# Reordering the second routing front of a hybrid block: row numbers, slots' experts, shared expert and clock fillers

## The chip, the core and the metric

The kernel runs on one core of a Trainium2 chip. The metric is device time in microseconds; the time before is the median of three runs. The core has a matrix engine (TensorE, "PE" in the profile), VectorE ("DVE"), ScalarE ("ACT"), GpSimd ("POOL") and SyncE ("SP"), which issues most DMAs. Each runs its own list of instructions in order, and they wait for one another by semaphores.

## The reference

A batch of 2 sequences of 1024 tokens with 128 channels passes through four residual steps. What is computed, cut to its core:

```python
x = x + attn_a(layernorm(x))   # RWKV-like linear attention
x = x + ffn(layernorm(x))      # first expert layer
x = x + attn_b(layernorm(x))   # hierarchical attention, 16 heads of 64
x = x + ffn(layernorm(x))      # second expert layer, the same weights

def ffn(x):
    shared_out = (silu(x @ shared_gate_w) * (x @ shared_up_w)) @ shared_down_w
    logits = x @ gate_w                      # 32 experts
    topk_ids = argmax(logits)
    xs = x * sigmoid(max(logits))
    sorted_x = xs[argsort(topk_ids)]         # tokens grouped by expert
    d = (silu(sorted_x @ gate_e) * (sorted_x @ up_e)) @ down_e
    return shared_out + d[inverse order]
```

## The kernel before, in words

Tokens lie in four chunks of 512 (c = 0 to 3), each of four tiles of 128. The kernel runs four stages in a row on every engine: `a_*`, the first expert layer `f_*` with k = 0, `b_*`, and the second expert layer `f_*` with k = 1. Each stage is a hand-written list per engine, so the order of the work is the order of the calls in the code.

Stage b takes 16 units (`UNITS`; a unit is a pair of heads of one sequence; `LAST` is 15). Per unit TensorE computes scores in two parts (fine and coarse, `scores`, L1755), VectorE subtracts maxima and transposes (`soften`, L2021), ScalarE takes exponents (L1935, L1939), TensorE forms the weighted sums (`weighted`, L1804) and their weights' sums (L1785 in the last unit), VectorE takes reciprocals (`divide`, L2038 to L2045), ScalarE copies the numerators (`copy_y`, L1954), GpSimd multiplies the two (L2204, two halves of 512 columns), TensorE projects (`project_out`, L1825), and VectorE adds the projection to the tokens (`gather_out`, L2054). The last two units are added in one gather per half.

The second expert layer has a front that overlaps the end of stage b. Chunks 0 and 1 are ready early and are routed during stage b. Chunks 2 and 3 come with the last unit. Per chunk: statistics on VectorE (`front_statistics`, L967 to L974), a power on GpSimd (L178), normalised rows (chunk 2 on ScalarE, L987; chunk 3 on VectorE, L1365), turns on TensorE (`front_turn`, L997), copies on ScalarE (L1002), logits (`front_logits`, L1007) and the choice of the expert on VectorE (`route`, L1026 to L1033), which writes a one-hot table. TensorE counts tokens from that table (`count_tokens`, L1090 and L1091).

Rows of tokens are then scattered into `sorted_x` in DRAM, grouped in slots of 32 rows per expert. The row numbers come in two halves of eight tiles, both on VectorE. For chunks 0 and 1 these are `first_slots` (L1109 to L1113) and `first_rows` (L1117, L1118, then L1099 to L1101). For chunks 2 and 3 it is `second_places` (L1125 to L1135, again L1099 to L1101). Its end (L1137 to L1143) finds the expert of each slot. GpSimd issues 16 indirect DMAs (`scatter`, L1469): eight wait for the first half's numbers, eight for the second's. When all 16 have landed, SyncE reads slots back (L1525). TensorE turns the rows (`turn_in`, L1197) and starts the loop over 24 steps of four slots (`gate_up`, L1251, and on).

Among all this lies the shared expert: `shared_half` (L1156, two matmuls of 512 columns on TensorE), `gate_shared` (L1172, ScalarE), `product_shared` (L1178, VectorE), `shared_out` (L1165, 16 matmuls) and `add_shared` (L1183, VectorE), for each chunk. The loop's first turn stands behind the last of it in TensorE's list. `keep_clock` (L1193) issues matmuls whose results nobody reads.

The order on VectorE in front of the loop is: `divide`, `first_slots`, gather, statistics, gather, statistics, `row_ids` (L1073), `first_rows`, chunk 3's rows, two products of chunk 0, `route` of chunks 2 and 3 in one call, `add_shared` of chunk 0, `second_places` with the slots' experts, two products of chunk 1, slot numbers. On TensorE it is: last projection, two shared halves of chunk 0, turns of chunks 2 and 3, logits of both, `shared_out` of chunk 0, `count_tokens`, two shared halves of chunk 1, `keep_clock(2)`, a shared half of chunk 2, the slots' row (L1218), and the rest of the shared expert.

Of the kernel before, what the change touches and what calls it, by code (L numbers as in the profile page):

```python
# [51 lines left out]
SLOT_BOUND = "second_places keeps the expert of a slot between 0 and EXPERTS - 1"  # L52
# [38 lines left out]
def hybrid_block(nc, w, out):  # L91
    with ExitStack() as ctx:
# [1028 lines left out]
        def second_places(dve, chain, k):  # L1121
# [14 lines left out]
            row_numbers(dve, chain, a, 1)  # L1136
            chain(dve.tensor_scalar(before.cmp[:, 0:EXPERTS], before.taken, place_col[:, 1:2], None, ALU.is_le))  # L1137
# [47 lines left out]
        def f_pe(pe, k):  # L1185
# [20 lines left out]
            else:  # L1206
                front_turn(pe, k, 2)
                front_turn(pe, k, 3)
                front_logits(pe, k, 2)
                front_logits(pe, k, 3)  # L1210
                shared_out(pe, k, 0)
            count_tokens(pe, k, 1)
            shared_half(pe, k, 1, 0, 1)
            shared_half(pe, k, 1, 1, 2)
            keep_clock(2)
# [70 lines left out]
        def f_act(act, k):  # L1286
# [5 lines left out]
            if k == 0:  # L1292
                front_copy(act, k, 3)
            else:
                gate_shared(act, k, 0, 0)
                front_norm(act, k, 2)
                gate_shared(act, k, 0, 1)
                front_copy(act, k, 2)
                front_copy(act, k, 3)
# [50 lines left out]
        def f_dve(dve, chain, k):  # L1350
# [8 lines left out]
            else:  # L1359
                row_ids(dve, k)  # L1360
                first_rows(dve, chain, k)
# [6 lines left out]
            if k == 1:  # L1368
                for n in range(2):
                    product_shared(dve, k, 0, n)  # L1370
                route(dve, chain, k, 2, 2)
# [5 lines left out]
            add_shared(dve, k, 0)  # L1377
            second_places(dve, chain, k)
            for n in range(2):
                product_shared(dve, k, 1, n)  # L1380
# [206 lines left out]
        for b in range(BATCH):  # L1587
# [8 lines left out]
            "acc logits_in").split()}  # L1596
# [95 lines left out]
        def b_pe(pe):  # L1692
# [8 lines left out]
            def keep_busy(times):  # L1701
                for _ in range(times):
                    pe.matmul(Y[0], ident, const[:, 0:CHUNK], start=True, stop=True)

# [113 lines left out]
            def project_out(n):  # L1818
                pe.wait_ge(wo_in[n % 2], 16 * (n // 2) + 16)
                for i in range(SEQ // P):  # L1820
                    if i % 4 == 0:
                        pe.wait_ge(h["normed"], 2 * n + i // 4 + 1)
# [22 lines left out]
            for n in range(UNITS + 1):  # L1845
# [7 lines left out]
                if new:  # L1853
# [3 lines left out]
                    project(n + 1, 1, 1)  # L1857
                if now:
                    scores(n, ROUGH)
                if new:  # L1860
# [26 lines left out]
                else:  # L1887
                    project_out(n - 1)
                    pe.wait_ge(h["y_out"], UNITS)
                    for half in range(2):  # L1890
                        shared_half(pe, 1, 0, half)
# [107 lines left out]
        def b_dve(dve, chain):  # L1999
# [48 lines left out]

            def gather_out(n, j):
# [39 lines left out]
            for n in range(0, UNITS + 1):  # L2089
# [14 lines left out]
                if n == UNITS:  # L2104
                    first_slots(dve, chain, 1)
# [278 lines left out]
```

## Time and profile before

| | us |
|---|---|
| median of three runs | 557.3 (556.14 to 558.34) |
| profiled execution, its own time | 555.4 |
| span of that execution in the trace | 553.5 |

All moments below are microseconds from the span's start. In a timeline the first two numbers are the start and the length of an instruction (or of a group of neighbours, with their count behind x); in brackets stand the idle time of the engine before it and what ended it. In the chain of waits each piece follows from the one above it.

### The profile page before, as it was taken

What the parts mean: (1) busy time and instruction counts of PE and PEld (TensorE: products, weight loads), DVE (VectorE), ACT (ScalarE), POOL (GpSimd) and SP (SyncE); (2) the same over time, 40 slices, a digit from 0 to 9 for tenths busy, and PEclk for the clock granted to TensorE, in tenths of its full rate; (3) what the DMA queues carried; (4) which work ended last, traced back from release to release, by engine and by line L of the source; (5) the groups of instructions that cost most, each with busy time, mean ns of one, the idle gap of its engine ahead of it and who ended that gap; (6) DMA issues with size and microseconds to landing.
All of it is one profiled execution on the core that took longest, in us unless ns stands there. A gap on an engine that the chain in (4) does not pass through costs nothing.

```text
span 553.5 us, 16703 instructions
## 1 busy us (share of the span) xinstructions
PE 497.8 (90%) x6472; PEld 306.0 (55%) x6472; DVE 422.3 (76%) x979; ACT 290.9 (53%) x624; POOL 250.7 (45%) x294
## 2 busy tenths in 40 slices
PE   6989888887989988999999999999999868989991
PEld 3323232355445544777767777777767656544540
DVE  3386968987757776878898888899878987747762
ACT  3544344254358864656545555546644433448870
POOL 3556777555614454253344443333233434534442
PEclk9999999999999998999999999999999987899997
DMA  6799820000269962100000000000000000169964
GB/s 183 313 426 285 95 26 0 2 0 20 81 195 271 279 203 68 31 3 21 21 21 22 23 21 22 22 21 21 22 21 8 7 2 16 37 191 275 277 215 139
DMA packets 45326, 54.11 MB, mean 98 GB/s; under 512 B 10880, under 2 KB 36416, under 8 KB 44224
## 3 DMA queue, kind: packets, MB, share of 16 engines
q1 hardware_dynamic: 42688, 47.78, 29.7%
q0 software_dynamic: 2560, 5.26, 2.7%
q8 instruction: 52, 0.85, 0.6%
q14 instruction: 26, 0.21, 0.2%
HBM read 43.55 MB, written 9.48 MB: 96 GB/s over the span
## 4 chain that ended last, share of the span: by engine, by line
PE 61%; DVE 23%; issue 6%; DMA 3%; POOL 3%; ACT 3%; SPq 0%; DVEq 0%; POOLq 0%; ACTq 0%
PE psum L1251 9%; PE psum L1732 7%; PE psum L1750 7%; PE psum L1825 5%; PE psum L1804 4%; PE psum L1270 4%; PE psum L1258 3%; DVE arena L761 3%; POOL sorted_x L1469 2%; PE psum L1773 2%; DVE arena L755 2%; PE psum L277 2%; PE psum L278 2%; DVE arena L2034 2%; DVE arena L2029 2%
## 5 line engine op out<-in xcount | busy, mean ns | idle before, releaser
L2204 POOL TENSOR_TENSOR arena<-arena 128x512 f32<-128x512 f32 x32 | 40.9, 1301 | 108.7 <-issue 102.1
L1497 POOL DMA_INDIRECT y_tok<-arena,to x48 | 46.4, 967 | 64.0 <-ACT arena L1320 62.8
L1920 ACT ACTIVATE arena<-psum 128x512 f32<-128x512 f32 x64 | 37.9, 597 | 45.2 <-PE psum L1732 42.0
L1732 PE MATMUL psum<-arena 128*128 128x512 f32 x128 | 59.2, 605 | 0.8 <-ACT arena L1903 0.7
L1251 PE MATMUL psum<-experts,arena 128*32 x96 | 50.2, 605 | 1.0 <-ACT arena L1310 1.0
L1251 PE MATMUL psum<-arena 128*32 128x512 f32 x288 | 50.9, 605 | 0.0
L661 POOL TENSOR_TENSOR arena<-arena 128x512 f32<-128x512 f32 x32 | 37.2, 1179 | 26.2 <-DVE arena L761 17.5
L1750 PE MATMUL psum<-arena 128*128 128x128 f32 x384 | 47.5, 279 | 1.5 <-ACT arena L1925 1.5
L1750 PEld LDWEIGHTS psum<-arena 128*128 128x128 f32 x384 | 45.2, 192 | 2.5 <-ACT arena L1925 2.5
L2141 POOL TENSOR_TENSOR arena<-arena 128x256 f32<-128x256 f32 (+4 forms) x75 | 33.8, 451 | 24.6 <-ACT arena L1939 17.9
L1732 PEld LDWEIGHTS psum<-arena 128*128 128x128 f32 x128 | 23.0, 190 | 35.5 <-issue 34.0
L1334 ACT ACTIVATE arena<-experts 128x768 f32 x48 | 40.1, 839 | 2.0 <-issue 1.8
L1393 DVE COPY arena<-psum 128x256 f32<-128x256 f32 x48 | 20.4, 425 | 25.4 <-PE psum L1258 25.0
L1469 POOL DMA_INDIRECT sorted_x<-arena,row x32 | 31.1, 970 | 19.3 <-DVE row L1101 10.7
L761 DVE TENSOR_TENSOR_SCAN arena<-psum,arena 128x512 f32<-128x512 f32 x32 | 39.1, 1269 | 0.0
L1804 PE MATMUL psum<-arena 64*64 64x64 f32 (+2 forms) x1728 | 37.1, 225 | 2.2 <-ACT arena L1935 1.5
L1928 ACT ACTIVATE arena<-psum 128x512 f32<-128x512 f32 x48 | 28.7, 598 | 16.4 <-PE psum L1750 16.4
L1270 PEld LDWEIGHTS psum<-experts,arena 128*32 128x32 f32 x192 | 20.6, 110 | 30.1 <-issue 29.8
L1804 PEld LDWEIGHTS psum<-arena 64*64 64x64 f32 x1728 | 33.2, 138 | 6.3 <-ACT arena L1935 1.6
L1825 PE MATMUL psum<-arena 128*128 128x128 f32 x256 | 34.4, 288 | 2.3 <-POOL arena L2204 2.3
L2054 DVE TENSOR_TENSOR x_tok<-x_tok,psum 128x512 f32<-128x512 f32 x30 | 20.6, 687 | 20.4 <-PE psum L1825 20.2
L755 DVE TENSOR_TENSOR arena<-arena,psum 128x512 f32<-128x512 f32 x32 | 19.9, 685 | 19.2 <-PE psum L293 19.1
(240 smaller groups left out, 1204.7 us busy)
## 6 DMA issues: line engine op xcount, KB each, us to landing
arena<-in_experts SPq DMA_DIRECT2D x48, 384.0 KB, 4.2
experts<-in_experts SPq DMA_DIRECT2D x8, 1536.0 KB, 17.3
arena<-sorted_x SPq DMA_DIRECT2D x48, 64.5 KB, 3.6
sorted_x<-zeros SPq DMA_DIRECT2D x2, 1536.0 KB, 13.7
arena<-in_w_qkv SPq DMA_DIRECT2D x16, 192.0 KB, 3.2
arena<-y_tok SPq DMA_DIRECT2D x8, 256.0 KB, 3.1
x_tok<-in_x SPq DMA_DIRECT2D x4, 256.0 KB, 4.5
arena<-in_w_out SPq DMA_DIRECT2D x16, 64.0 KB, 1.9
```

Source lines behind the costliest of these rows:

```text
L761: dve.tensor_tensor_scan(a_state[:, m, 1:CHUNK + 1], DECAYS[:, :], a_kv[m % HALF], a_state[:, m, 0:1], ALU.mult, ALU.add).then_inc(s["stat ...
L1251: mm = pe.matmul(bank[2 + s % 2][rows, :], f_gxt[s % 2][:, rows], weights, start=True, stop=True)
L1270: mm = pe.matmul(bank[6 + s % 2][SLOT_ROWS * j:SLOT_ROWS * j + SLOT_ROWS, 0:C], f_sht[s % 2][:, rows], weights, start=(half == 0), stop=(h ...
L1334: act.activation(f_w_act[s % 5], experts[:, bass.ds(expert_at[s], WROW)], ACT.Copy).then_inc(t["w_act"], 1)
L1469: pool.indirect_dma_start(out=sorted_x[k], out_offset=bass.IndirectOffsetOnAxis(ap=f_row[:, i:i + 1], axis=0), in_=row_of(k, i), in_offset ...
L1497: pool.indirect_dma_start(out=y_tok, out_offset=bass.IndirectOffsetOnAxis(ap=f_to[:, s:s + 1], axis=0), in_=f_gy[(s + 4) % 8], in_offset=N ...
L1732: pe.matmul(ring("in", n, j)[:, :], b_w[n % 2][:, which * P:which * P + P], x, start=True, stop=True)\
L1750: mm = pe.matmul(ring("in", n, 5 + i // 4)[:, i % 4 * P:i % 4 * P + P], x, b_w[n % 2][:, 2 * P:3 * P], start=True, stop=True)
L1804: mm = pe.matmul(place(Y[r][out]), b_v[n % 2][rows, i, out], e[rows, head, i - part.start, cols], start=(i == 0), stop=last_place(r, i, cols))
L1825: mm = pe.matmul(ring("out", n, i // 4)[:, i % 4 * C:i % 4 * C + C], b_yn[:, i * P:i * P + P], b_wo[n % 2], start=(n < LAST - 1 or n < LAS ...
L1920: act.activation((b_q, b_k)[which][:, part * CHUNK:part * CHUNK + CHUNK], src, ACT.Copy, scale=(D_B ** -0.5, 1.0)[which]).then_inc(h["drai ...
L2204: pool.tensor_tensor(b_yn[:, part], b_y[:, part], b_rec[:, part], ALU.mult).then_inc(h["normed"], 1)
```

## The change

Only the second front (k = 1) and the last unit of stage b change their order. For k = 0 the calls stay as they were.

- TensorE: fillers (matmuls whose results nobody reads) ahead of and behind the last unit's coarse scores. The last projection stands between the two shared halves of chunk 0, with three fillers behind. Turn and logits come chunk by chunk. A shared half of chunk 1 stands ahead of the counting, `shared_out` of chunk 0 behind it. `keep_clock` goes.
- VectorE: it normalises the second half of the last unit in place of GpSimd (`normalise_late`), and takes a product of chunk 0 there. `first_slots` moves behind the statistics, `first_rows` behind chunk 3's rows. After the routing come one product, `second_places`, `slot_experts` (cut out of `second_places`), and only then the add of chunk 0 and the products of chunk 1.
- ScalarE: the second gate of chunk 0 ahead of chunk 2's rows.
- GpSimd: one multiply less in the last unit.

The diff, without two lines that only rename and some context:

```diff
@@ second_places
             row_numbers(dve, chain, a, 1)
+
+        def slot_experts(dve, chain, k):
+            before, a = half_of(k, 0), half_of(k, 1)
             chain(dve.tensor_scalar(before.cmp[:, 0:EXPERTS], before.taken, place_col[:, 1:2], None, ALU.is_le))
...
@@ f_pe
             else:
                 front_turn(pe, k, 2)
+                front_logits(pe, k, 2)
                 front_turn(pe, k, 3)
-                front_logits(pe, k, 2)
                 front_logits(pe, k, 3)
+                shared_half(pe, k, 1, 0, 1)
+            count_tokens(pe, k, 1)
+            if k == 0:
+                shared_half(pe, k, 1, 0, 1)
+            else:
                 shared_out(pe, k, 0)
-            count_tokens(pe, k, 1)
-            shared_half(pe, k, 1, 0, 1)
             shared_half(pe, k, 1, 1, 2)
-            keep_clock(2)
+            if k == 0:
+                keep_clock(2)
             shared_half(pe, k, 2, 0)
             done(pe, "slot_col", 1)
@@ f_act
                 gate_shared(act, k, 0, 0)
+                gate_shared(act, k, 0, 1)
                 front_norm(act, k, 2)
-                gate_shared(act, k, 0, 1)
                 front_copy(act, k, 2)
@@ f_dve
                 row_ids(dve, k)
-                first_rows(dve, chain, k)
...
             ins.then_inc(t["xn_last"], 1)
             if k == 1:
+                first_rows(dve, chain, k)
+                route(dve, chain, k, 2, 2)
+                product_shared(dve, k, 0, 1)
+                second_places(dve, chain, k)
+                slot_experts(dve, chain, k)
+                add_shared(dve, k, 0)
                 for n in range(2):
-                    product_shared(dve, k, 0, n)
-                route(dve, chain, k, 2, 2)
+                    product_shared(dve, k, 1, n)
             else:
                 route(dve, chain, k, 2, 1)
                 for n in range(2):
                     product_shared(dve, k, 0, n)
                 route(dve, chain, k, 3, 1)
-            add_shared(dve, k, 0)
-            second_places(dve, chain, k)
-            for n in range(2):
-                product_shared(dve, k, 1, n)
+                add_shared(dve, k, 0)
+                second_places(dve, chain, k)
+                slot_experts(dve, chain, k)
+                for n in range(2):
+                    product_shared(dve, k, 1, n)
@@ b_pe
+            def fill_wait(cols):
+                for at in range(0, cols, CHUNK // 2):
+                    pe.matmul(ring("out", LAST - 1, 0)[:, 0:CHUNK // 2], ident, const[:, 0:CHUNK // 2], start=True, stop=True)
@@ project_out
                     if i % 4 == 0:
-                        pe.wait_ge(h["normed"], 2 * n + i // 4 + 1)
+                        if n == LAST and i:
+                            pe.wait_ge(h["normed_late"], 1)
+                        else:
+                            pe.wait_ge(h["normed"], 2 * n + i // 4 + 1)
@@ b_pe, loop over units
+                if n == LAST:
+                    pe.wait_ge(h["acc"], 2 * (LAST - 1))
+                    fill_wait(CHUNK + CHUNK // 2)
                 if now:
                     scores(n, ROUGH)
+                if n == LAST:
+                    fill_wait(CHUNK)
...
                 else:
+                    pe.wait_ge(h["y_out"], UNITS)
+                    shared_half(pe, 1, 0, 0)
                     project_out(n - 1)
-                    pe.wait_ge(h["y_out"], UNITS)
-                    for half in range(2):
-                        shared_half(pe, 1, 0, half)
+                    shared_half(pe, 1, 0, 1)
+                    pe.wait_ge(h["z_out"], UNITS)
+                    for _ in range(3):
+                        pe.matmul(bank[7], ident, const[:, 0:CHUNK], start=True, stop=True)
@@ b_dve
+            def normalise_late():
+                part = slice(CHUNK, SEQ)
+                dve.wait_ge(h["y_out"], UNITS)
+                dve.wait_ge(h["o"], 2 * LAST)
+                dve.tensor_tensor(b_yn[:, part], b_y[:, part], b_rec[:, part], ALU.mult).then_inc(h["normed_late"], 1)
@@ b_dve, loop over units
                 if n == UNITS:
-                    first_slots(dve, chain, 1)
+                    normalise_late()
+                    product_shared(dve, 1, 0, 0)
...
                     route(dve, chain, 1, n - PAIRS - 4, 1)
+            first_slots(dve, chain, 1)
             dve.wait_ge(h["acc"], 2 * LAST)
@@ b_pool_engine
-                for j in range(2):
+                for j in range(2 if n < LAST else 1):
```

## Rows read from the trace of the kernel before

**Rows 1.** The page, part 4: shares of the chain that ended last, by engine.

```profile
PE 61%; DVE 23%; issue 6%; DMA 3%; POOL 3%; ACT 3%; SPq 0%; DVEq 0%; POOLq 0%; ACTq 0%
```

**Rows 2.** Chain of waits in order of time, 479 to 495: start, length, what.

```profile
479.02 0.18 DVE row L1101
...
488.88 2.68 DMA sorted_x<-arena,row
...
494.25 0.31 PE psum L1197
```

**Rows 3.** Timeline of GpSimd, 454 to 481: start, length, line, operation, [idle before].

```profile
454.48 2.91 POOL L2204 TENSOR_TENSOR arena<-arena 128x512 f32<-128x512 f32 x2 [2.23 <-DVE arena L2045]
...
462.90 1.25 POOL L178 TENSOR_TENSOR arena<-arena,const 128x4 f32<-128x4 f32 x1 [1.18 <-DVE arena L974]
465.91 1.10 POOL L1469 DMA_INDIRECT sorted_x<-arena,row  x1 [1.77 <-DVE row L1101]
...
474.90 0.97 POOL L1469 DMA_INDIRECT sorted_x<-arena,row  x1 [0.30 <-issue]
480.03 0.96 POOL L1469 DMA_INDIRECT sorted_x<-arena,row  x1 [4.16 <-DVE row L1101]
```

**Rows 4.** Timeline of VectorE, 458 to 482.

```profile
458.41 0.69 DVE L2054 TENSOR_TENSOR x_tok<-x_tok,psum 128x512 f32<-128x512 f32 x1
...
462.86 0.42 DVE L1117 TENSOR_TENSOR arena<-arena 128x256 f32<-128x256 f32 x1
...
464.96 1.11 DVE L1365 TENSOR_SCALAR arena<-x_tok,arena 128x128 f32<-128x128 f32 x4
...
469.65 0.42 DVE L1026 TENSOR_REDUCE arena<-psum 128x8 f32<-128x256 f32 x1 [2.40 <-PE psum L1007]
...
473.90 0.19 DVE L1125 TENSOR_TENSOR psum<-psum,arena 128x32 f32<-128x32 f32 x1
...
477.44 0.43 DVE L1135 TENSOR_TENSOR arena<-arena 128x256 f32<-128x256 f32 x1
...
480.36 1.29 DVE L1178 TENSOR_TENSOR arena<-arena,psum 128x512 f32<-128x512 f32 x2
```

**Rows 5.** Lines L1109 and L1094 over the span: min, median, max in ns.

```profile
L1109 DVE TENSOR_TENSOR_SCAN arena<-const,psum x1: 689/689/689, 124.0 to 124.0; 128x256 f32<-128x256 f32 x1
L1109 DVE TENSOR_TENSOR_SCAN arena<-const,arena x1: 1331/1331/1331, 455.0 to 455.0; 128x256 f32<-128x256 f32 x1
...
L1094 DVE TENSOR_SCALAR arena<-arena x4: 189/190/1096, 124.7 to 474.9; 128x32 f32<-128x32 f32 x4
```

**Rows 6.** Timeline of TensorE, 443 to 494 (an fp32 matmul stands as two).

```profile
443.92 0.30 PE L1767 MATMUL psum<-attend_bf 64*64 64x256 bf16 x4 [1.59 <-DVE arena L2029]
...
446.20 3.26 PE L1804 MATMUL psum<-arena 64*64 64x64 f32 x103 [1.51 <-ACT arena L1935]
...
455.90 3.62 PE L1825 MATMUL psum<-arena 128*128 128x128 f32 x16 [2.29 <-POOL arena L2204]
...
464.06 0.66 PE L997 MATMUL psum<-const,arena 128*128 128x128 f32 x4 [0.66 <-ACT arena L987]
...
469.43 3.76 PE L1165 MATMUL psum<-shared_down,arena 128*128 128x128 f32 x16
...
477.11 1.88 PE L1193 MATMUL psum<-shared_up,const 128*128 128x512 f32 x4
...
481.70 2.05 PE L1165 MATMUL psum<-shared_down,arena 128*128 128x128 f32 x16 [0.69 <-DVE arena L1178]
...
493.42 0.31 PE L1197 MATMUL psum<-const,arena 128*128 128x128 f32 x1
```

**Rows 7.** Busy time by stretch: PE, PEld, DVE, ACT, POOL, then granted clock, DMA share, GB/s.

```profile
446.80:450.00 3.20, 3.06 (x107) 2.87 (x105) 3.10 (x6) 0.81 (x3) 0.28 (x1) 0.50 0.02 5
...
467.20:474.00 6.80, 6.80 (x31) 6.42 (x31) 2.88 (x8) 3.38 (x9) 5.16 (x6) 0.50 0.16 55
```

**Rows 8.** Timeline of ScalarE at 452.

```profile
452.35 1.02 ACT L1954 ACTIVATE arena<-psum 128x1024 f32<-128x1024 f32 x1 [4.40 <-POOL arena L2204]
```

More of the change, by code:

```diff
@@ L51 @@
 FOUND = 4
-SLOT_BOUND = "second_places keeps the expert of a slot between 0 and EXPERTS - 1"
+SLOT_BOUND = "slot_experts keeps the expert of a slot between 0 and EXPERTS - 1"
 ROW = C + 1
@@ L1595, in hybrid_block @@
             "shift xn xt x pooled packed packed_odd ready coarse proj drained scored subbed turned expd weighed merged summed y_out z_out divided normed o biased "
-            "acc logits_in").split()}
+            "acc logits_in normed_late").split()}
         w_in, wo_in, bias_in = [sem(f"b_w_in{r}") for r in range(2)], [sem(f"b_wo_in{r}") for r in range(2)], sem("b_bias_in")
```

## Prediction

> **What bounds the kernel now.** I read the page first: TensorE heads the chain that ended last [rows 1], yet the change touches only the stretch between the last attention unit (from about 442 us) and the start of the second expert loop (495 us). The loop behind it runs at one pace per slot, so what counts is when it starts. The profiled execution took 555.4 us for a span of 553.5 us; the median of the runs is 557.3 us, 1.9 above it. Differences are worked out on the span and taken off the median.
>
> Followed backwards, the loop starts when a slot's rows have been read back; that waits for the last of 16 scatters, landed 2.68 us after its issue; and the second eight scatters waited for the second half's row numbers, written at 479.02 [rows 2]. GpSimd stood idle for 4.16 us ahead of them, at 480.03. A scatter takes 1.26 us (eight starts from 465.91 to 474.90, the first 0.15 longer) [rows 3]. TensorE reached the first slot's turn at 493.42, 0.8 us ahead of the turn at 494.25 that waited for the read-back [rows 2, 6]. Two chains of almost equal length end here, **scatters** and **shared expert**: the change pays only if both get shorter.
>
> **Last unit.** TensorE runs at 0.50 of its clock (the 1.2 GHz level) from 446.8 to 450.0, behind a hole in which it waited 1.59 us for VectorE and one of 1.51 us for ScalarE [rows 6, 7]. The added fillers (three of 256 columns ahead of the coarse scores, two behind) sit in these holes. Two of 512 columns took 1.88 us [rows 6], so a 256 one is about 0.47: 1.4 and 0.9 us, less than either hole. They cost nothing while the clock is full; at half clock the first three would take 2.8 us and push the scores back by 1.2. If the clock stays full, 3.2 us of work at half rate could shrink by up to 1.6, and the last divide comes earlier. But ScalarE's copy of the last numerators (452.35, 1.02 us) waits for GpSimd, not for this work [rows 8]: behind it, at 453.4, TensorE now does the first shared half (two 512 matmuls, 1.88 us at most) and starts the last output projection at 455.2 instead of 455.90 [rows 6]. I take **0.7 us** (ends 0 and 0.7; above it the copy binds).
>
> **Gathers.** Today the first half's slot counts lie on VectorE between its divide and the first gather at 458.41, though the projection's first half was there at about 457 [rows 4, 6]. The change puts the late normalise and one shared product there (0.65, half of the two in 1.29 [rows 4]; the normalise has no row: 0.65 as the nearest of its shape on VectorE, 1.45 as one of GpSimd's two in 2.91 [rows 3]; I take 0.65, and with either it is done ahead of the projection's second half at 456.2). Half of 16 matmuls of that shape at 2.05 us [rows 6] puts the first gather at 456.25: **2.16 us earlier** (1.46 if the 0.7 fails). From there to the end of the row ids, with the second gather and the statistics, it is 4.45 us today (458.41 to 462.86) [rows 4].
>
> Behind the projection TensorE does the second shared half (to about 459.1) and three fillers of 512 columns (2.8 us at 0.94 each, to 461.9). Chunk 2's turn, at 464.06 today, waits for ScalarE's rows and comes due 2.16 earlier, at 461.9 [rows 6]: nothing lost at full clock, up to 3 us of lateness for the logits at half clock. ScalarE's second gate moves ahead of those rows; its input is there from 458.2 and the shift it now precedes comes at 460, so it costs nothing.
>
> **Slot counts and first row numbers.** The counts now stand between the statistics and the row ids. In the second front they took 3.44 us beside a GpSimd multiply; the first front shows their scan at 0.69 instead of 1.33 and the first small operation at 0.19 instead of 1.10 [rows 5]. Without the multiply that is 3.44 - 0.64 - 0.91 = 1.9 us; its ends are 1.9 and 3.44, and I take 1.9, as only a short GpSimd power is beside it. So the row ids end at 456.25 + 4.45 + 1.9 = 462.6. Then the last chunk's rows, 1.11 us [rows 4]: 463.7, **2.35 us earlier** than 466.07. Then the first row numbers, 2.10 (462.86 to 464.96): 465.8, **0.85 us later** than today.
>
> What that power (1.25 us from 462.90) does to VectorE the trace shows: the 256-wide add at 462.86 took 0.42 us beside it, and the one at 477.44, with GpSimd idle, 0.43 [rows 3, 4]. I charge nothing. Against this stands a rule: the Trainium skill, GPSIMD Engine Reference, section Specifications, says that GpSimd shares its SBUF interfaces with VectorE, with contention for VectorE instructions in a two-port mode or with two SBUF inputs. By that rule the moved counts could lose some 0.65 us beside the power, an estimate, and the sum would be 0.65 us worse; the rows beside the multiply bear it out, the add beside the power does not.
>
> **Scatters.** GpSimd starts 0.95 us after the row numbers (464.96 to 465.91) [rows 3, 4]: 466.75. Nothing separates the two eights now, if the second row numbers come in time: the last of 16 starts 1.41 + 14 x 1.263 = 19.1 us later, at 485.85, against 488.88 [rows 2, 3]: **3.0 us earlier**. Landing and read-back stay as they are; the weight loads ahead of them move along.
>
> Do the second row numbers come in time? With turns and logits of chunks 2 and 3 one by one, chunk 3's turn starts at about 464.2 behind chunk 2's logits (TensorE's order, where today VectorE's rows set it), and its own logits end at about 466.6; today both sets, partly at half clock, hold VectorE until 469.65 [rows 4, 7]. The two-chunk routing (2.35 us, 469.65 to 472.0) ends at 469.0. Its call still takes both chunks at once: "one by one" holds for turns and logits alone. Counting no longer waits behind the shared output (3.76 us from 469.43 [rows 6]); the second places start at 469.65, behind one shared product, and take 5.2 (473.90 to 479.1) [rows 2, 4]: 474.9, so that GpSimd could issue at 475.8. It is busy with the first eight until 477.0. So **1.2 us of slack**: late next is the queue of GpSimd, not the routing.
>
> **Shared expert.** Slots' experts 1.25, one add 0.69, two products 1.29: the second product ends at 478.1 instead of 481.65 [rows 4], and the second shared output starts then instead of at 481.70, 3.6 earlier. The 11.7 us behind it (to 493.42) keep their order and end at 489.8; the scatters then bind, at 494.25 - 3.0 = 491.25 [rows 2, 6]. The two clock fillers that go (1.88 us, hidden in a wait) leave TensorE with hardly any work from 475.1 to 478.1. A half-clock stretch costs half its length: 3.2 us cost 1.6, 6.8 us (467.2 to 474.0) cost 3.4 [rows 7]. The 1.45 us between the two chains cover the first but for 0.15, not the second. Ends 0 and 3.4; I charge nothing.
>
> **Sum.** 3.0 us off: span 550.5, execution 552.4, median 557.3 - 3.0 = **554.3 us**. A measurement of this kernel tells about 0.5% (2.8 us) from no change, so the forecast lies just beyond that edge. Its own range: 552.8 (landing quicker, as fewer weight loads are in flight) to 555.9 (slot counts at their upper end, 1.55 more).
>
> **Rivals.**
> First, **the front stays slow**: the clock gains nothing (0.7) or the counts stay at 3.44 (1.55), or both. The row numbers come up to 2.25 us later, and all 16 scatters with them: 555.0 to 556.5. For it: the slow rows lie beside GpSimd work, and some is left. Against: the first front's rows. Chance 0.2.
> Second, **the shared chain ends last**, because the clock falls in the 3 us hole that the fillers left: with 3.4 us lost TensorE is at its first turn at 493.2, 0.2 earlier than today, so 557.1; with 1.6 to 2.5 lost 554.5 to 556.2. For it: the stretch from 467.2 to 474.0. Against: the other low stretch lasted 3.2 us. Chance 0.17.
> Third, **slower**: the same fall, but the low clock reaches into the loop, whose matmuls then run another 6.8 us at half rate, 3.4 us lost on top of the second rival's end: 560.5. It decides once the low stretch lasts past the loop's start at 491.9. For it: with 6.8 us behind 478 the clock is back only 7 us ahead of that, and a hole of its own may follow. Against: both of today's low stretches ended under dense work, and the shared expert's from 481.70 on is dense [rows 6, 7]. Chance 0.1.
> Fourth, more than forecast: both chains short and the landing quick: 552.2. Chance 0.08.
>
> **How the numbers follow.** The forecast has 0.45. The range 552.0 to 557.6 leaves out the slower case and some tail below. Faster by over 0.5% (under 554.5): two thirds of the forecast's case, the fourth, and the mild ends of the first two, 0.42; slower by over 0.5%: 0.11, the third and a little of what no case names; within: 0.47.
>
> **What would show it.** Right: the granted clock stays full from 446 to 460; the first gather at about 456.3; slot counts in 1.9 us; the first scatter at about 466.8 and sixteen without a pause, the last at 485.9; TensorE's second turn waiting for the read-back, the loop starting about 492. Wrong: a pause in the scatters (routing late), a first scatter after 468, half clock behind 477, or turns that no longer wait for data. If the loop's own pace changes, the sum is void.

## The result and the profile after

The changed kernel takes 554.49 us (median of 6 runs, 553.68 to 555.91) beside 557.54 us for the kernel before on the same chip: a ratio of 0.9949, 95% interval [0.9928, 0.9971]. The forecast was 554.3 us, so the time is right. The trace shows that part of the way there was another one. One of all the executions below, of the kernel called e12, was slow (639.32 us at a granted clock of 0.748), and its median and ratio leave that one out.

The profiled execution after took 554.11 us for a span of 552.2 us (555.4 and 553.5 before). I measure the **front** from the start of the last unit's coarse scores (443.92 before, 444.07 after) to the loop's first `gate_up` (494.98 before, 493.51 after): 51.06 us became 49.44 us. The stretch behind it is 58.5 us before and 58.7 us after.

Shares of the chain that ended last, as in [rows 1]:

```profile
PE 64%; DVE 21%; issue 7%; ACT 3%; DMA 3%; POOL 2%; DVEq 0%; POOLq 0%; SPq 0%; ACTq 0%
```

The chain of waits of the kernel after, in order of time (start, length, what), to set beside [rows 2]:

```profile
465.79 1.16 PE psum L1007 x8
466.95 3.41 PE psum L1159 x4
470.36 0.11 PE psum L1090
...
475.85 0.17 DVE row L1101
...
477.78 1.29 DVE arena L1181 x2
...
479.11 2.72 PE psum L1168 x16
481.84 4.43 PE psum L1159 x8
486.27 1.78 PE psum L1168 x16
...
492.67 0.11 PE psum L1200
492.78 0.31 PE psum L1200
```

Before, the scatters, their landing and the read-back stood at the end. None of them is in this chain. TensorE's shared expert (L1159, L1168) runs through to the first turns (L1200) with no wait for a DMA. The other chain is still close: SyncE issues the read-back at 490.36, 1.2 us earlier than before, and the first slot's rows land some 1.8 us later, just ahead of the turns at 492.50.

GpSimd after, beside [rows 3]:

```profile
453.75 1.28 POOL L2239 TENSOR_TENSOR arena<-arena 128x512 f32<-128x512 f32 x1 [1.34 <-PE psum L1844]
...
461.05 1.31 POOL L178 TENSOR_TENSOR arena<-arena,const 128x4 f32<-128x4 f32 x1 [1.18 <-DVE arena L974]
466.98 1.08 POOL L1481 DMA_INDIRECT sorted_x<-arena,row  x1 [4.62 <-DVE row L1101]
...
473.43 1.19 POOL L1481 DMA_INDIRECT sorted_x<-arena,row  x1 [0.30 <-issue]
...
477.56 0.96 POOL L1481 DMA_INDIRECT sorted_x<-arena,row  x1 [0.30 <-issue]
...
486.42 0.96 POOL L1481 DMA_INDIRECT sorted_x<-arena,row  x1 [0.30 <-issue]
```

The 4.16 us pause between the two eights is gone: 477.56 is the ninth scatter. The first starts 1.07 us later than before, the last 2.46 us earlier (486.42 against 488.88 in [rows 2]).

VectorE after, beside [rows 4] and [rows 5]:

```profile
454.24 1.34 DVE L2080 TENSOR_TENSOR arena<-arena 128x512 f32<-128x512 f32 x1
455.60 0.69 DVE L1181 TENSOR_TENSOR arena<-arena,psum 128x512 f32<-128x512 f32 x1
456.56 0.69 DVE L2087 TENSOR_TENSOR x_tok<-x_tok,psum 128x512 f32<-128x512 f32 x1 [0.27 <-PE psum L1844]
...
460.88 0.69 DVE L1109 TENSOR_TENSOR_SCAN arena<-const,arena 128x256 f32<-128x256 f32 x1
461.60 0.19 DVE L1094 TENSOR_SCALAR arena<-arena 128x32 f32<-128x32 f32 x1
...
462.76 0.23 DVE L1073 TENSOR_SCALAR arena<-const,place_col 128x8 f32<-128x8 f32 x1
462.90 1.11 DVE L1371 TENSOR_SCALAR arena<-x_tok,arena 128x128 f32<-128x128 f32 x4
...
466.99 0.42 DVE L1026 TENSOR_REDUCE arena<-psum 128x8 f32<-128x256 f32 x1 [0.88 <-PE psum L1007]
...
470.62 0.20 DVE L1125 TENSOR_TENSOR psum<-psum,arena 128x32 f32<-128x32 f32 x1 [0.58 <-PE psum L1091]
```

The gather waits 0.27 us for TensorE's projection, not for VectorE's own work. The counts take 1.88 us (460.88 to 462.76) where they took 3.44. The routing starts at 466.99, not at 469.65.

ScalarE's copy of the last numerators after, beside [rows 8]:

```profile
452.50 1.02 ACT L1981 ACTIVATE arena<-psum 128x1024 f32<-128x1024 f32 x1 [4.40 <-POOL arena L2239]
```

TensorE after, beside [rows 6], and its granted clock, beside [rows 7] (busy time of PE, PEld, DVE, ACT and POOL, then clock, DMA share, GB/s):

```profile
446.35 1.16 PE L1820 MATMUL psum<-arena 64*64 64x64 f32 x64 [0.28 <-ACT arena L1962]
...
455.40 1.95 PE L1844 MATMUL psum<-arena 128*128 128x128 f32 x16
457.18 1.88 PE L1159 MATMUL psum<-arena,shared_up 128*128 128x512 f32 x4
458.90 2.74 PE L1918 MATMUL psum<-const 128*128 128x512 f32 x6
...
466.76 3.60 PE L1159 MATMUL psum<-arena,shared_up 128*128 128x512 f32 x4
...
479.11 2.72 PE L1168 MATMUL psum<-shared_down,arena 128*128 128x128 f32 x16 [1.41 <-DVE arena L1181]
481.63 4.64 PE L1159 MATMUL psum<-arena,shared_up 128*128 128x512 f32 x8
```

```profile
446.00:450.00 4.00, 3.08 (x180) 2.87 (x183) 3.86 (x7) 1.11 (x4) 0.12 (x1) 1.00 0.01 4
450.00:466.00 16.00, 13.62 (x116) 9.03 (x107) 14.35 (x45) 6.59 (x11) 6.02 (x5) 1.00 0.00 1
...
467.00:470.00 3.00, 3.00 (x4) 1.07 (x5) 2.76 (x6) 0.60 (x4) 2.39 (x3) 0.50 0.11 39
...
480.30:481.00 0.70, 0.70 (x6) 0.70 (x6) 0.00 (x0) 0.00 (x0) 0.70 (x1) 0.50 0.29 94
...
483.00:483.70 0.70, 0.70 (x2) 0.34 (x1) 0.00 (x0) 0.12 (x1) 0.58 (x1) 0.50 1.02 315
```

The fillers sit in what were holes, and the clock is full from 446 to 466. It is at 0.50 (the 1.2 GHz level) from about 467 to 470, and once more from 480.3 to 483.7. The second stretch follows the place where `keep_clock` stood until the change: TensorE waits 1.52 us ahead of the slots' row (477.32) and 1.41 us ahead of the second `shared_out` (479.11), and the clock falls 1.2 us into that.

### The profile page after: what moved, and what is told of

Same layout as the page of the kernel before. It is cut to its first block, busy times and chain, and to the rows that moved or that the text cites. A ratio compares the mean times of both kernels' runs of the same rounds, so it can differ in the third digit from the quotient of the medians.

```text
span 552.2 us, 16726 instructions
## 1 busy us (share of the span) xinstructions
PE 496.9 (90%) x6484; PEld 303.2 (55%) x6484; DVE 422.4 (76%) x980; ACT 291.0 (53%) x624; POOL 249.2 (45%) x293
## 4 chain that ended last, share of the span: by engine, by line
PE 64%; DVE 21%; issue 7%; ACT 3%; DMA 3%; POOL 2%; DVEq 0%; POOLq 0%; SPq 0%; ACTq 0%
PE psum L1258 9%; PE psum L1766 7%; PE psum L1748 7%; PE psum L1844 5%; PE psum L1820 4%; PE psum L1277 4%; PE psum L1265 3%; DVE arena L761 3%; PE psum L1789 3%; DVE arena L755 2%; PE psum L277 2%; PE psum L1159 2%; PE psum L278 2%; PE psum L1168 2%; DVE arena L2105 2%
## 5 line engine op out<-in xcount | busy, mean ns | idle before, releaser
L2239 POOL TENSOR_TENSOR arena<-arena 128x512 f32<-128x512 f32 x31 | 39.2, 1285 | 108.0 <-issue 102.4
L661 POOL TENSOR_TENSOR arena<-arena 128x512 f32<-128x512 f32 x32 | 37.2, 1181 | 26.2 <-DVE arena L761 17.5
L1766 PE MATMUL psum<-arena 128*128 128x128 f32 x384 | 47.5, 278 | 1.5 <-ACT arena L1952 1.5
L1820 PE MATMUL psum<-arena 64*64 64x64 f32 (+2 forms) x1728 | 35.9, 221 | 1.5 <-ACT arena L1966 1.2
L1844 PE MATMUL psum<-arena 128*128 128x128 f32 x256 | 33.0, 281 | 0.4 <-issue 0.4
```

The lines of the kernel that those rows point to most:

```text
L661: pool.tensor_tensor(a_g[m % HALF], a_r[c % 2], a_state[:, m, 0:CHUNK], ALU.mult).then_inc(s["g"], 1)
L1766: mm = pe.matmul(ring("in", n, 5 + i // 4)[:, i % 4 * P:i % 4 * P + P], x, b_w[n % 2][:, 2 * P:3 * P], start=True, stop=True)
L1820: mm = pe.matmul(place(Y[r][out]), b_v[n % 2][rows, i, out], e[rows, head, i - part.start, cols], start=(i == 0), stop=last_place(r, i, cols))
L1844: mm = pe.matmul(ring("out", n, i // 4)[:, i % 4 * C:i % 4 * C + C], b_yn[:, i * P:i * P + P], b_wo[n % 2], start=(n < LAST - 1 or n < LAS ...
L2239: pool.tensor_tensor(b_yn[:, part], b_y[:, part], b_rec[:, part], ALU.mult).then_inc(h["normed"], 1)
```

## Experiments

For each kernel the table gives moments of one profiled execution, in us from the start of the last unit's coarse scores ("front" is the loop's start), and the time of the runs with its ratio to the kernel before on the same chip. The rows were timed on several chips, where the medians of the kernel before lay between 556.92 and 557.54 us. So a cost between two rows is taken from their ratios below; as each ratio has an interval of about 0.2% to either side, such a cost is uncertain by some 1.5 us.

| kernel | first scatter | second row numbers end | last scatter starts | read-back issued | shared expert ends | front | median, ratio [interval] |
|---|---|---|---|---|---|---|---|
| before | 21.99 | 35.27 | 44.96 | 47.66 | 49.66 | 51.06 | |
| e1 before | 22.08 | 35.21 | 44.90 | 47.51 | 49.60 | 50.92 | |
| e11 before | 22.08 | 35.20 | 44.89 | 47.71 | 49.59 | 50.90 | |
| after | 22.91 | 31.95 | 42.35 | 46.29 | 48.59 | 49.44 | 554.49, 0.9949 [0.9928, 0.9971] |
| e2 after | 22.91 | 32.10 | 42.47 | 45.71 | 48.72 | 49.28 | |
| e5 first rows back | 21.89 | 34.74 | 44.42 | 49.28 | 51.39 | 52.40 | 556.89, 1.0 [0.9988, 1.0012] |
| e6 no unit fillers | 23.71 | 32.75 | 43.13 | 45.96 | 49.39 | 50.11 | 555.74, 0.9992 [0.9973, 1.0011] |
| e10 no wide fillers | 22.92 | 34.49 | 44.18 | 47.65 | 49.46 | 50.80 | 556.27, 0.999 [0.9971, 1.0009] |
| e3 `keep_clock` back | 22.94 | 31.71 | 42.10 | 45.76 | 46.68 | 48.86 | 553.53, 0.9944 [0.9926, 0.9962] |
| e4 a weight load later | 22.90 | 31.94 | 42.33 | 45.12 | 48.57 | 49.13 | 554.39, 0.995 [0.9933, 0.9967] |
| e7 both of these | 22.92 | 31.95 | 42.34 | 44.62 | 46.92 | 47.89 | 553.66, 0.9942 [0.9924, 0.996] |
| e8 GpSimd normalises | 22.92 | 31.13 | 42.01 | 44.72 | 46.10 | 47.92 | 553.31, 0.9934 [0.9914, 0.9955] |
| e12 the same again | 22.91 | 33.21 | 42.90 | 47.41 | 48.18 | 50.69 | 554.23, 0.995 [0.993, 0.9971] |
| e9 three edits | 22.91 | 31.13 | 41.99 | 45.17 | 47.09 | 48.35 | 554.28, 0.9951 [0.9932, 0.997] |

**Both kernels once more (e1, e2, e11).** The times fell by 3.05 us, the front of the profiles by 1.6. Does the front vary, or does something ahead of it?

> The kernel of before, unchanged, profiled a second time. Its first profile (555.4 us) lies below all its timed runs (556.1 to 558.8), while that of the changed kernel (554.1) lies among its own (553.7 to 555.9). If the trace of before that the prediction used was simply a lucky one, this profile comes out at 556 to 558 us, with more low-clock time than 0.974 allowed, most of it between 442 and 495 us (theory A: the change removes clock losses that vary from run to run). If before's runs differ elsewhere (theory B: another stage, or the time around the span), the stretch 442 to 495 is the same within 0.5 us and the difference lies outside it.

> The changed kernel a second time. Theory A: the stretch from 442 us to the loop's start repeats within 1 us, as its clock is held by fillers up to 466. Low-clock stretches behind 466 and behind 479 should be there again, perhaps shifted. Time 553.7 to 555.9 us.

> The kernel before once more, for a third profile. The front between the last unit's coarse scores and the loop took 51.06 and 50.92 us in two profiles of it, and 49.44 and 49.28 in two of the kernel after, 1.6 us apart, while the timed medians lie 2.5 to 3 apart. If the rest is the spread of what lies ahead of the front, the front repeats within 0.2 us and the coarse scores start somewhere between 443.9 and 445.8; if the front itself varies, it shows 52 or more.

Measured: the front of the kernel before repeats within 0.16 us in three executions, that of the kernel after within 0.16 us in two. The coarse scores start at 443.92, 445.30 and 445.77 in the kernel before, at 444.07 and 444.52 in the kernel after, and up to 446.03 in the others, whose code ahead of them is the same. So what lies ahead moves by some 2 us from execution to execution, and the front's own 1.6 us is clear of the spread of these five profiles. (The pair e8 and e12 below shows a larger spread.)

**The first row numbers back to their place (e5).**

```diff
                 row_ids(dve, k)
+                first_rows(dve, chain, k)
...
             if k == 1:
-                first_rows(dve, chain, k)
                 route(dve, chain, k, 2, 2)
```

> The changed kernel with the first half's row numbers back ahead of chunk 3's rows on VectorE. Working from the changed kernel's rows: the row numbers move 1.0 us earlier (to about 465.1 us), chunk 3's rows 2.1 us later, the routing and the second row numbers 1.5 to 2.1 later (478.0). If the forecast's account is right (16 scatters in a row, 1 to 1.5 us of slack for the routing), the first scatter starts 1.0 earlier, a pause of 1.5 to 2.0 us comes between the eights, and the last scatter starts within 0.7 us of the changed kernel's, later rather than earlier. The shared expert's chain moves 1.5 to 2.0 later and ends last: time 1 to 2 us above the changed kernel's. Rival: if the early start of the first eight is what counts, the last scatter starts 1 us earlier and the time falls by up to 1 us.

Measured: 556.89 us at a ratio of 1.0, the whole gain gone. The two rows of TensorE for chunk 3's turn and logits in e5, and GpSimd's scatters:

```profile
466.12 1.12 PE L997 MATMUL psum<-const,arena 128*128 128x128 f32 x4 [1.54 <-DVE arena L1372]
467.92 1.91 PE L1007 MATMUL psum<-gate_w,arena 128*128 128x32 f32 x8 [0.69 <-ACT arena L1002]
```

```profile
474.90 0.95 POOL L1481 DMA_INDIRECT sorted_x<-arena,row  x1 [0.30 <-issue]
479.61 0.95 POOL L1481 DMA_INDIRECT sorted_x<-arena,row  x1 [3.76 <-DVE row L1101]
```

The first scatter is 1.0 us earlier and the ninth 2.1 us later. Chunk 3's rows come behind the numbers, TensorE waits 1.54 us for them, and behind that wait the clock is at 0.51 (466 to 470), so that turn and logits take nearly twice as long. I had expected the last scatter to lose at most 0.7 us, and it lost 2.1; the clock was left out of that. Against the coarse scores chunk 3's turn starts 1.7 us later than in the kernel after and its logits end 2.9 us later: 1.7 are the order, the other 1.2 the clock, and the run does not part the two in the time. In this profile the read-back is issued 4.86 us after the last scatter (3.94 after), so its front of 52.40 is not the order's alone either. Still, this is the part on which the change rests: a later first eight for an earlier second eight.

**Without the fillers of the last unit (e6).**

```diff
-                if n == LAST:
-                    pe.wait_ge(h["acc"], 2 * (LAST - 1))
-                    fill_wait(CHUNK + CHUNK // 2)
                 if now:
                     scores(n, ROUGH)
-                if n == LAST:
-                    fill_wait(CHUNK)
```

> The changed kernel without the fillers around the last unit's coarse scores. The forecast gave them 0.7 us (0 to 0.7). If right: half clock from about 447 to 450 again, the last sum 0.8 us later, the last projection's start 0 to 0.7 us later (the copy of the numerators binds otherwise), and the first scatter as much later. Rival: nothing moves behind the projection, as the copy and the first shared half set it in either case; then the fillers are worth nothing here: no change in the scatters' start beyond 0.1 us.

TensorE in e6:

```profile
447.27 1.55 PE L1820 MATMUL psum<-arena 64*64 64x64 f32 x64 [1.51 <-ACT arena L1957]
...
457.04 2.02 PE L1844 MATMUL psum<-arena 128*128 128x128 f32 x16 [0.54 <-POOL arena L2234]
```

The 1.51 us hole is back, the clock averages 0.62 from 446.9 to 450.9 (as far behind the coarse scores as 446 to 450 in the kernel after, where it is 1.00), and the projection starts 12.05 behind the coarse scores instead of 11.33. These 0.72 us go on to the loop (50.11 against 49.36, the mean of the two profiles after). By the ratios (0.9992 for 0.9949) the runs lose 2.4 us, more than this front shows, though not beyond the uncertainty.

**Without the three wide fillers (e10).**

```diff
                     shared_half(pe, 1, 0, 1)
-                    pe.wait_ge(h["z_out"], UNITS)
-                    for _ in range(3):
-                        pe.matmul(bank[7], ident, const[:, 0:CHUNK], start=True, stop=True)
```

> The kernel after without the three 512-column fillers behind the last projection and the second shared half. Theory that they hold the clock: the granted clock falls between 461 and 467, turns and logits come later (second choice of the expert by 0.5 to 2 us), the first scatter stays at 22.9 behind the coarse scores, the shared expert ends later or at the same time; time 0 to 1 us above the kernel after. Theory that they only cost TensorE's time: turn 2 and the logits keep their starts, since ScalarE's rows set them, the clock is full there anyway, and the time stays within 0.5.

TensorE's timeline and its stretches in e10:

```profile
464.17 0.66 PE L997 MATMUL psum<-const,arena 128*128 128x128 f32 x4 [3.14 <-ACT arena L987]
465.51 1.91 PE L1007 MATMUL psum<-gate_w,arena 128*128 128x32 f32 x8 [0.69 <-ACT arena L1002]
...
470.74 3.76 PE L1159 MATMUL psum<-arena,shared_up 128*128 128x512 f32 x4
```

```profile
460.00:464.00 4.00, 1.02 (x3) 0.19 (x1) 3.73 (x21) 2.13 (x5) 2.02 (x2) 1.00 0.00 0
464.00:468.00 4.00, 3.15 (x16) 2.84 (x16) 3.76 (x13) 0.71 (x2) 0.31 (x1) 0.59 0.00 0
468.00:472.00 4.00, 3.31 (x12) 2.47 (x11) 1.05 (x4) 1.88 (x2) 2.44 (x3) 0.50 0.09 31
```

Behind the 3.14 us wait the clock falls for the whole routing: both sets of logits take 1.91 us instead of 1.08 and 1.16, and the second row numbers come 2.5 us later than in the kernel after. The first scatter stays (22.92), a 2.2 us pause between the eights is back, and the runs are at 0.999 of before, by the ratios 2.3 us above the kernel after where 0 to 1 was expected. That is not one profile's chance: the mean granted clock of each of its ten executions is 0.968 to 0.980, of the six of the kernel after 0.981 to 0.984. The theory that these fillers hold the clock stands; that they only take TensorE's time falls.

**The clock fillers back, a weight load later, and both (e3, e4, e7).**

```diff
-            if k == 0:
-                keep_clock(2)
+            keep_clock(2)
```

```diff
-            for s in range(4):
+            for s in range(4 - k):
...
                 fetch(s)
+                if k == 1 and s == 3:
+                    weights(3)
```

> The changed kernel with the two clock fillers of the second front put back (between chunk 1's second shared half and chunk 2's first). Theory S (the shared expert ends last, because TensorE's clock falls in the hole from 475 to 479 us): full clock behind 479, the first slot's turn 1.0 to 1.7 us earlier, and the time 0.3 to 1.2 us less than the changed kernel's, as the read-back follows closely. Theory R (the scatters and the read-back end last): the first turn comes earlier too, but the loop does not start earlier by more than 0.3 us, as the second turn then waits for data; no change in time.

> The changed kernel with the fourth of the four weight loads that SyncE issues ahead of the scatters' wait moved behind the first four read-backs, in the second front alone. The last scatter landed 3.9 us after its issue in the changed kernel and 2.7 in the one before. If the weight loads in flight cause that, three quarters of their bytes should let the last scatter land 0.8 to 1.3 us earlier. Theory S: the loop's start does not move by more than 0.3 us, since the shared expert ends last. Theory R: it starts 0.5 to 1.2 us earlier, and so does the end.

> The changed kernel with both edits of the last two experiments: the two clock fillers back and the fourth weight load behind four read-backs. The fillers alone let the shared expert end 1.1 us ahead of the data; the later load alone let the last scatter land 0.8 us earlier but the shared expert ended last. If the two chains bind in turn, together they give what neither gave alone: first turn about 0.8 us earlier than with the fillers alone, loop start 1.2 to 1.5 us ahead of the changed kernel's, time 0.5 to 0.9 us below that with the fillers alone. If something else binds (the slots' weights, say), no less than with the fillers alone.

TensorE in e3, from the second `shared_out` on:

```profile
479.07 2.05 PE L1168 MATMUL psum<-shared_down,arena 128*128 128x128 f32 x16 [1.02 <-DVE arena L1181]
480.96 3.60 PE L1159 MATMUL psum<-arena,shared_up 128*128 128x512 f32 x8
...
491.93 0.78 PE L1200 MATMUL psum<-const,arena 128*128 128x128 f32 x2 [0.98 <-DMA arena<-sorted_x]
```

2.05 and 3.60 us instead of 2.72 and 4.64: the clock is full there, the shared expert ends 1.9 us earlier than after, and the turn waits for the read-back again. So in the kernel after, with `keep_clock` gone and the clock low, the shared expert ended last. But the front gains only 0.5 us of it, because the read-back is next. One pair of profiles doesn't settle that the removal brings the fall: without `keep_clock` the clock fell there in five profiles (after, e2, e4, e5, e6) and stayed at 1.00 in three (e8, e10, e12), behind waits of 1.0 to 1.6 and 1.41 us in all of them; with it, it stayed in all three (e3, e7, e9). In e4 the read-back was issued 0.6 to 1.2 us sooner and the loop's start hardly moved (49.13): shared expert again. That sooner read-back is what the theory of the weight loads asked for (2.79 us after the last scatter, and 2.28 in e7, against 3.94, 3.24 and 3.66 in after, e2 and e3). But e6 and e8, with all four loads ahead, have 2.83 and 2.71, so it isn't shown that the load did it. With both edits the front is 47.89, 1.5 us shorter than after. One step of the loop then took 2.58 us where 1.92 is usual, so that from the coarse scores to the end 1.0 us is left (107.2 for 108.1); the span shows none of it (552.6 for 552.2), as what lies ahead took 1.4 us longer in that execution. Of the three, no time can be told from that of the kernel after.

**GpSimd normalises the second half again (e8, e12).**

```diff
-                        if n == LAST and i:
-                            pe.wait_ge(h["normed_late"], 1)
-                        else:
-                            pe.wait_ge(h["normed"], 2 * n + i // 4 + 1)
+                        pe.wait_ge(h["normed"], 2 * n + i // 4 + 1)
...
-                    normalise_late()
...
-                for j in range(2 if n < LAST else 1):
+                for j in range(2):
```

> The changed kernel with the last unit's second half normalised by GpSimd again, as in the kernel before; all else stays. The late normalise took VectorE 1.34 us beside GpSimd's multiply (twice the 0.65 that the forecast took), and VectorE then still waited 0.27 us for the projection. If VectorE's list is what sets the first gather, the gather comes 0.2 us earlier or so at most; GpSimd's second half ends at about 456.3, when TensorE has just done the projection's first half, so the second gather is not later either: no change (within 0.3 us) in the first scatter's start. Rival: GpSimd's second half comes late by its usual 1.3 to 1.45 us, the projection waits, and the second gather and all behind it come up to 0.7 us later.

> Once more the kernel after with GpSimd normalising the last unit's second half. In six kernels with that multiply on VectorE TensorE waits 0.57 us ahead of chunk 2's turn and the granted clock falls behind chunk 3's logits; in the two with it on GpSimd the wait is 0.40 to 0.43 and the clock stays full up to the loop. Theory that the multiply's place decides this: the clock is 1.00 from 466 to 484 again, the second row numbers come 31.1 behind the coarse scores (31.95 in the kernel after), the loop starts 47.7 to 48.4 behind them, and the time is 553 to 553.8. Theory that the two were chance: the clock falls between 466 and 470, row numbers at 31.7 or later, loop 49 or later, time 554 to 555.

The first scatter stands at 22.92 and 22.91, as after: the multiply's move to VectorE is worth nothing to it. In e8 the clock stayed full from 466 to 484, and I took that for the edit's doing. The second execution says otherwise. Chunk 3's logits and the last landing in e8:

```profile
467.42 1.08 PE L1007 MATMUL psum<-gate_w,arena 128*128 128x32 f32 x8 [0.69 <-ACT arena L1002]
```

```profile
487.72 2.69 DMA sorted_x<-arena,row
```

and in e12, the same code:

```profile
466.17 1.92 PE L1007 MATMUL psum<-gate_w,arena 128*128 128x32 f32 x8 [0.69 <-ACT arena L1002]
```

```profile
487.36 4.49 DMA sorted_x<-arena,row
```

The stretch from 466 to 472, first e8, then e12 (the clock is the third figure from the end):

```profile
466.00:472.00 6.00, 4.37 (x24) 2.54 (x24) 4.82 (x12) 2.89 (x6) 2.75 (x3) 1.00 0.07 23
466.00:472.00 6.00, 5.83 (x15) 3.52 (x16) 3.31 (x8) 2.79 (x8) 3.71 (x4) 0.50 0.11 34
```

The same instructions in the same order gave fronts of 47.92 and 50.69. The difference is a clock of 0.50 from 466 to 472 and a landing that took 1.8 us longer. So the multiply's place alone doesn't decide it. What does stays open: the profiled execution of e12 was the slowest of its eleven (557.03 us, median 554.23), but the mean granted clock is 0.984 to 0.986 in all four executions of e8 and 0.978 to 0.984 in the eleven of e12, on another chip. In the twelve executions of e9, on one chip, it is 0.978 to 0.987, so that executions of one program on one chip differ as much; whether the chip adds to that is not shown.

**Three edits together (e9).** GpSimd normalises, `keep_clock` is back, and the slot numbers stand ahead of chunk 1's products:

```diff
                 add_shared(dve, k, 0)
+                slot_numbers()
                 for n in range(2):
```

> The kernel after with three edits: GpSimd normalises the second half again, the two clock fillers behind the counting are back, and the slot numbers stand ahead of chunk 1's two products on VectorE, so that SyncE's weight loads start about 1.2 us earlier. Theory S (behind the change the shared expert's chain ended last, and with the fillers back the read-back does): the scatters stay as they are, the last 42.2 to 42.4 us behind the last unit's coarse scores; the weight loads are done before the last scatter lands, which then takes 2.8 us or less; the loop starts 47.5 to 47.9 behind those scores (49.44 in the kernel after) and the time is 552.5 to 553.3. If the loop's tail pays back what the front gains (as one look had it, 0.66 us), 553.3 to 554. Theory that the landing is set by the scatters themselves and not by the weight loads beside them: landing stays above 3 us, the loop starts at 48.3 or later.

Measured: 554.28 us and a front of 48.35, where 47.5 to 47.9 was expected; by its ratio this version can't be told from the kernel after. The weight loads were issued 1.28 us earlier against the coarse scores (34.86 for 36.14) and the landing still took 3.16 us. The theory that the loads beside it set the landing has no support in this run.

## Why the prediction was right, and where it was not

**The last unit, 0.7 us: right.** The projection starts at 455.40 (455.2 forecast), 0.65 us earlier against the coarse scores than before; without the fillers 0.72 us are lost. ScalarE's copy stands at 452.50, 8.43 us behind the coarse scores as in the kernel before [rows 8]: it is what caps this gain, as the text said.

**The gather at 456.25: 456.56.** The normalise was taken as 0.65 and took 1.34 us, beside GpSimd's multiply (453.75 to 455.03). That is the direction of the rule weighed in the prediction (the Trainium skill, GPSIMD Engine Reference, Specifications). The longer normalise cost nothing: the gather waited for the projection, as the text said for either value, and starts at the same distance in e8.

**The counts, 3.44 to 1.9 us: 1.88, right.** Here that rule does not show: the scan takes 0.69 us and the small operation 0.19 with GpSimd's power beside them (461.05, 1.31 us). The scan began 0.17 us ahead of that power, the small operation within it. The first numbers and the first scatter (466.98 for 466.75) carry on only the gather's 0.3 us.

**Sixteen scatters without a pause: right,** though the last starts at 486.42, not at 485.85: 0.23 us from the start, the rest mostly from two issues of 1.19 and 1.08 us. The slack of the second places was 0.6 us rather than 1.2, since their end came at 476.02, not 474.9. The low clock from 467 to 470 had eaten into it through `count_tokens`, which stands behind a shared half of 3.60 us (466.76) where e8 shows 1.97.

**The three wide fillers, "nothing lost": half right.** They cost nothing, but the step put their worth at nothing too. The forecast's logits at 466.6 hang on them: without them the runs lose some 2.3 us.

**The clock behind the removed `keep_clock`, charged at nothing (ends 0 and 3.4): wrong.** This term failed, and it is rival 2's mechanism. Two of the text's own signs of being wrong came with it: half clock behind 477, and turns that no longer wait for data. The second `shared_out` was to start at 478.1 and started at 479.11, as the second places came late. From there the low stretch added 0.67 us (2.72 for 2.05) and 1.04 us (4.64 for 3.60). The first turn, forecast at 489.8, came at 492.50: 2.7 us late, more than the 1.45 us between the chains. (Rival 2's upper price is too high: with 3.4 us lost the first turn at 493.2 is 1.95 us behind the forecast's 491.25, so about 556.3 by the sum's own measure and not 557.1, and the third rival's 560.5 falls by as much.)

**Landing unchanged at 2.68 us: wrong in the profiled execution.** From the last issue to the read-back it is 3.94 us, and 3.24 in e2. Over all kernels it is 2.28 to 4.86 us, and 2.71 and 4.51 in one and the same kernel (e8, e12). What sets it stays open.

**The other rivals.** The front did not stay slow (clock full from 446 to 466, counts 1.88), so the first falls. The third's low clock in the loop's beginning is not there: the clock is 1.00 from 493.51 to 497.5, and the stretch behind the front kept its length within 0.2 us. It can come: in e12 the clock is 0.54 from 496 to 498 and 0.61 from 498 to 500, inside the loop, and that stretch takes 60.0 us. The fourth's quick landing did not come.

**The sum.** With both, the front gained 1.6 us where 3.0 were summed. The median fell by 3.05 us, 2.5 against the median of 557.03 us over 19 other runs of the kernel before. So the forecast time was hit in part by luck: two terms of the sum failed, and about 1 us of the timed gain is in no profile. It is no more than what a profiled execution differs from the next in this family (2.8 us between e8 and e12), and 1.6 us lies inside the ratio's interval at its end of 0.9971. Settling it would take many profiles of both kernels; it stays open.

The parts don't add up: taken away singly, first rows, wide fillers and unit fillers cost 2.8, 2.3 and 2.4 us by the ratios, 7.5 together, against a gain of 2.8 by the same measure. Each opens a wait or a low clock on the same chain; that this hides what the others save is likely but not shown, as no run takes away two at once.

## What to carry to other kernels

Order two batches of numbers by what the second one waits for: the queue that consumes the first batch gives the second time, and a later start of the first costs less than a pause between them. When a filler on TensorE is removed or added, price the clock of the work behind it and not the filler's own time; here that was some 2.3 us for fillers that seemed free. And take a second profile of a kernel before explaining a front by one: two executions of the same code lay 2.8 us apart.

## What was unexpected in the hardware

- The granted clock is not fixed by the instructions' order. In e8 and e12 TensorE waited 0.40 and 0.41 us ahead of chunk 2's turn and 0.69 us ahead of either set of logits; then the clock stayed at 1.00 in the one and was 0.50 from 466 to 472 in the other. The two executions were on different chips.
- A VectorE multiply of 128x512 out of two SBUF tiles took 1.34 us beside a GpSimd multiply of that size; the product that follows it, with GpSimd idle and one operand in PSUM, took 0.69. The slow one ended 0.55 us behind the GpSimd multiply (455.58 for 455.03). Beside a GpSimd power of 128x4 a VectorE scan, begun just ahead of it, and four small operations begun within it lost nothing (0.69, and 0.18 to 0.22 us; the last three took the same in the kernel before with GpSimd idle).
- The last of 16 indirect scatters had landed, and the read-back was issued, 2.28 to 4.86 us after its own issue. The two kernels with one weight load fewer ahead of it had 2.79 and 2.28, but two executions of one program 2.71 and 4.51.
